# Turning the probabilities of the last self attention with ordinary matmuls instead of transposes

## The chip, the core and the metric

The kernel runs on one core of a Trainium2 chip. The metric is the device time of one execution in microseconds (us), as the median of several runs. TensorE (PE) runs the matmuls, VectorE (DVE), ScalarE (ACT) and GpSimd (POOL) the elementwise work, and DMA queues move data. PE's clock has two levels, 1.2 and 2.4 GHz; the profile gives the granted one as a share, 0.50 or 1.00, and between them as a mean over a stretch.

## What is computed

The reference is a pair of gated blocks on x [32, 100, 128] with a context [32, 1444, 128]. The last block is an attention of the tokens on themselves, a layernorm and a mixture of 8 experts. The attention is what matters here:

```python
q = (src @ Wq + bq).reshape(B, T, NHEAD, HEAD_DIM)      # T = 100, 16 heads of 8
scores = jnp.einsum('bqhd,bkhd->bhqk', q, k) * scale
probs = jax.nn.softmax(scores, axis=-1)
out = jnp.einsum('bhqk,bkhd->bqhd', probs, v).reshape(B, T, d)
return out @ Wo + bo
```

All of it is in float32.

## The kernel before

Three stages follow one another: stage A (the first block), stage B (cross attention to the context) and stage C (`stage_c`). Stage C is written by hand: each engine has its own program, and semaphores are the only tie between them. It first runs the self attention of 32 sequences and then the experts. The attention works in 8 units (`b`, 0 to 7) of 4 sequences; a sequence is two pieces of 8 heads, so there are 64 pieces (`k`) and 8 slots (`s` = `k % 8`) in a unit. A piece passes through these steps:

- PE `scores(k)` (L1801): two products of 400 columns, into one of two pairs of PSUM banks.
- DVE `subtract(k)` (L2018, L2022): the row maximum, and scores minus maximum into the tile `P`.
- ACT `exponent(k)` (L1640): exp in place in `P`.
- PE `turn_pieces(k)` (L1810): the eight 100x100 blocks of `P`, one a head, are turned into PSUM banks 4 and 5. It waits for exp of this piece and for the copy of the piece before.
- ACT `keep(k)` (L1646): one copy of all eight blocks to the tile `PT`.
- PE `weigh(k)` (L1822): eight products of `V` (with ones beside it, for the denominators) with `PT`.
- After every second piece ACT `outputs` (L1652) copies the result, PE `back` (L1847) turns it to tokens, and DVE `divide` (L2032, L2033) divides by the denominators.

PE's order in slot `s` is `scores(k + 2)`, `back` of the sequence before (even slots), `turn_pieces(k)`, one extra, `weigh(k)`. The extras prepare the next unit and finish the one before: slot 0 `gate` (L1754 on `c_YT`) and `attended` (L1766); slot 1 `turn1`; slot 2 `outer` (L1754 on `c_OT`); slot 3 `turn0` (L1749 on `c_H`); slot 4 `keys` (L1779); slot 5 `queries` (L1783); slot 6 `values` (L1754 on `c_HT`); slot 7 `turn2`. Unit 0 has none of the last unit's leftovers, unit 7 none of the next one's preparation.

ACT's order around it is `outputs`, `enter` (slot 3) or `middle` (slot 5, both four activations on L1603), `keep(k)`, `exponent(k + 1)`, then the copies of the extras. DVE's order is `divide`, `shift`, `subtract(k + 1)`, and `residual` (L2041) in slot 3. Every engine runs its list strictly in order.

`project` is the ordinary product of the kernel on four sequences, and `ident` is the identity:

```python
for j in range(GROUP):                                    # GROUP = 4
    last = mm(bank(b, T, width, j * width), lhsT[:, t.ts_(j)], rhs, start=True, stop=True)
```

Of the kernel before, what the change touches and what calls it, by code (L numbers as in the profile page):

```python
# [24 lines left out]
T = 100  # L25
# [1419 lines left out]
def stage_c(nc, t, x1, att, w1, w2, out):  # L1445

    with ExitStack() as ctx:
        def sb(name, shape, dt=F32):
            return ctx.enter_context(nc.sbuf_tensor("c_" + name, shape, dt))
# [4 lines left out]
        psum, K, tanhs, ident = t.psum, t.K, t.tanhs, t.ident  # L1454
        w, col, row, bank, tok_bank = t.w, t.col, t.row, t.bank, t.tok_bank
# [16 lines left out]
        P = sb("P", [T, 2, HQ // 2])  # L1472
# [271 lines left out]
        def _(pe):  # L1744
            mm = nc.tensor.matmul
# [59 lines left out]
            def turn_pieces(k):  # L1805
                pe.wait_ge(sem["fe_ready"], k + 1)
                if k:
                    pe.wait_ge(sem["fpT_ready"], k)
                for a in range(8):
                    x_ = nc.tensor.transpose(bank(4 + a // 4, T, T, (a % 4) * T), P[:, k % 2, t.ts_(a)], ident[0:T, 0:T])  # L1810
                x_.then_inc(sem["fpT_psum"], 1)

            def weigh(k):
# [114 lines left out]
            for k in range(PIECES):  # L1928
                b, s = divmod(k, SLOTS)
                if k + 2 < PIECES:  # L1930
                    scores(k + 2)
                if s % 2 == 0 and k:
                    back(k // 2 - 1)
                turn_pieces(k)
                if s == 0 and b >= 2:
                    gate(b - 2)
                if b < LAST:
                    if s == 0:
                        attended(b + 1)
                    if s == 3:  # L1940
                        turn0(b + 1)
                    if s == 4:
                        keys(b + 1)
                    if s == 5:
                        queries(b + 1)
                    if s == 6:
                        values(b + 1)
                if b:
                    if s == 1:
                        turn1(b - 1)  # L1950
                    if s == 2:
                        outer(b - 1)
                    if s == 7:
                        turn2(b - 1)
                weigh(k)
# [288 lines left out]
```

## Time and profile before

| | us |
|---|---|
| median of 3 runs (lowest, highest) | 2407.45 (2407.42, 2408.7) |
| the profiled execution's own time | 2401.97 |
| its span, first to last instruction | 2400.2 |
| PE busy | 2028.5 (85%) |
| DVE busy | 1583.8 (66%) |
| ACT busy | 1320.0 (55%) |
| L1810, matmul side: 512 instructions | 66.4 |
| stage C's attention loop, first turn to the last `back` | 1856.2 to 2154.4 |

An instruction group is told by its line, engine and operation and by output<-inputs; `psum<-K,c_P` is the turning of `P` with the identity, which lies in the constants `K`. A group's PE time is the busy time of overlapping instructions: eight turns in a row take 0.85 us together, though one lasts 249 ns. What stands in brackets behind a row is idle time of the engine before the row, with the instruction that ended it.

### The profile page before, as it was taken

The page shows a single profiled execution, that of the slowest core. Times are in us where ns is not written, and L with a number is a line of the kernel's source. Part 1 is how long each engine was busy: PE and PEld are TensorE (multiplying, and loading weights), DVE is VectorE, ACT ScalarE, POOL GpSimd, SP SyncE. Part 2 cuts the span into 40 slices and gives each one's busy share as a digit, 9 for nine tenths or more (in the row PEclk, how much of TensorE's full clock was granted, in tenths as well). Part 3 has the DMA queues.
Part 4 walks back from the last instruction along what each step waited for, and adds up shares of the span by engine and source line. Part 5 has one row for each costly group of instructions (what it writes and reads, how often), then busy time and mean ns, then how long its engine had stood idle before and what let it go on. Part 6 is the DMA issues. An engine that isn't in the chain of part 4 may idle for free. (4 is left out here: it accounts for less than half of the span.)

```text
span 2400.2 us, 45166 instructions
## 1 busy us (share of the span) xinstructions
PE 2028.5 (85%) x17914; PEld 1347.5 (56%) x17914; DVE 1583.8 (66%) x3854; ACT 1320.0 (55%) x2169; POOL 535.9 (22%) x476
## 2 busy tenths in 40 slices
PE   3779997466599999999999999999996888878997
PEld 2546665343355556556565555556564565656776
DVE  5844543787578878877877878878862566654443
ACT  3645554576246666666666666666673555543333
POOL 1410000553302212212222212212212233221111
PEclk9789997666589999999999999999997898879999
DMA  5026662000222313313323323313312110000000
GB/s 160 1 86 187 186 186 75 4 18 17 90 69 104 115 64 113 114 64 117 107 77 108 107 72 113 115 62 115 115 43 94 35 36 18 1 1 4 8 8 11
DMA packets 89104, 181.18 MB, mean 75 GB/s; under 512 B 5907, under 2 KB 63163, under 8 KB 88511
## 3 DMA queue, kind: packets, MB, share of 16 engines
q1 hardware_dynamic: 88894, 178.30, 22.6%
q8 instruction: 143, 2.34, 0.4%
q14 instruction: 67, 0.54, 0.1%
HBM read 95.24 MB, written 11.65 MB: 45 GB/s over the span
## 5 line engine op out<-in xcount | busy, mean ns | idle before, releaser
L1408 DVE TENSOR_REDUCE b_part_max<-psum 128x1 f32<-128x482 f32 (+3 forms) x1248 | 737.3, 650 | 187.6 <-PE psum L1285 173.6
L1198 ACT ACTIVATE b_PT<-psum 128x800 f32<-128x800 f32 x768 | 616.4, 836 | 386.0 <-PE psum L1304 380.0
L1285 PE MATMUL psum<-b_KH,b_QBD 64*128 64x482 f32 (+1 forms) x1152 | 421.4, 443 | 46.3 <-DVE b_part_max L1408 43.4
L1304 PE MATMUL psum<-b_QS,b_KS 64*128 64x200 f32 x3072 | 438.7, 288 | 0.5 <-ACT b_PT L1198 0.3
L1304 PEld LDWEIGHTS psum<-b_QS,b_KS 64*128 64x128 f32 x3072 | 339.6, 186 | 16.2 <-issue 12.1
L1320 PE MATMUL psum<-b_PT,b_V 128*32 128x200 f32 x6144 | 341.1, 339 | 0.6 <-ACT b_PT L1198 0.6
L1285 PEld LDWEIGHTS psum<-b_KH,b_QBD 64*128 64x128 f32 x1152 | 196.6, 188 | 198.0 <-DVE b_part_max L1408 118.6
L1121 POOL TENSOR_TENSOR b_KL<-b_KF,b_KH 128x1444 fp32r<-128x1444 f32 x32 | 106.8, 3337 | 691.9 <-PE psum L1304 669.7
L1320 PEld LDWEIGHTS psum<-b_PT,b_V 128*32 128x32 f32 x6144 | 159.9, 109 | 149.0 <-ACT b_PT L1198 82.3
L2096 DVE SCALAR_TENSOR_TENSOR c_U<-psum,c_gt,c_U 100x128 f32<-100x128 f32 x256 | 72.1, 344 | 129.0 <-PE psum L1917 128.8
L384 POOL TENSOR_TENSOR a_rs<-a_ve,a_half 100x4 f32<-100x4 f32 x48 | 50.0, 1041 | 420.7 <-DVE a_ve L757 420.6
L1917 PE MATMUL psum<-c_W,c_HE 128*100 128x128 f32 x1024 | 123.6, 274 | 14.1 <-ACT c_HE L1682 14.0
L1917 PEld LDWEIGHTS psum<-c_W,c_HE 128*100 128x100 f32 x1024 | 117.2, 167 | 31.8 <-ACT c_HE L1682 18.7
L1272 PE MATMUL psum<-W,b_CT 128*128 128x128 f32 (+1 forms) x768 | 117.7, 293 | 12.7 <-DVE b_part_max L1408 6.7
L804 DVE TENSOR_REDUCE a_peak<-psum 100x1 f32<-100x1446 f32 x32 | 53.2, 1664 | 105.3 <-PE psum L629 105.3
L1272 PEld LDWEIGHTS psum<-W,b_CT 128*128 128x128 f32 (+1 forms) x768 | 92.7, 188 | 41.4 <-DVE b_part_max L1408 37.4
L1682 ACT ACTIVATE c_HE<-psum,C 128x400 f32<-128x400 f32 x128 | 71.9, 587 | 78.9 <-PE psum L1906 75.9
L1646 ACT COPY c_PT<-psum 100x800 f32<-100x800 f32 x64 | 52.5, 821 | 102.0 <-PE psum L1810 102.0
L636 PE MATMUL psum<-a_P,a_CN 128*128 128x100 f32 (+1 forms) x768 | 108.0, 288 | 0.0
L1261 PE MATMUL psum<-b_CT,W 128*128 128x482 f32 (+1 forms) x192 | 101.2, 611 | 5.5 <-DVE b_QF L1382 1.5
L636 PEld LDWEIGHTS psum<-a_P,a_CN 128*128 128x128 f32 (+1 forms) x768 | 95.2, 195 | 18.7 <-issue 11.8
L1535 POOL TENSOR_TENSOR c_rs<-c_ve,c_half 100x4 f32<-100x4 f32 x24 | 24.4, 1015 | 337.0 <-DVE c_ve L1998 337.0
(274 smaller groups left out, 3204.3 us busy)
## 6 DMA issues: line engine op xcount, KB each, us to landing
b_KS<-b_KH SPq DMA_DIRECT2D x64, 722.0 KB
a_CT<-in_ctxt SPq DMA_DIRECT2D x32, 722.0 KB, 4.2
b_CT<-in_ctxt SPq DMA_DIRECT2D x32, 722.0 KB, 4.3
b_KS<-b_KL SPq DMA_DIRECT2D x32, 722.0 KB
a_CN<-in_ctxn SPq DMA_DIRECT2D x32, 704.0 KB
att_scratch<-b_AO SPq DMA_DIRECT2D x32, 200.0 KB, 1.9
c_AIN<-att_scratch SPq DMA_DIRECT2D x8, 800.0 KB
b_MB<-in_mask SPq DMA_DIRECT2D x32, 180.5 KB, 4.4
```

Source lines behind the costliest of these rows:

```text
L636: x_ = mm(bank(7, D, T, TG), CN[0:rows, m % 3, k, :], PTA[0:rows, m % 2, k, :], start=(k == 0), stop=(k == KT - 1))
L1121: pl.tensor_tensor(KL[:, :], KF[:, 0:S], KH[:, j % 2, :].bitcast(F32), ALU.subtract).then_inc(sem["kl_ready"], 1)
L1198: nc.scalar.activation(PT[:, kt % 2, 2 * a:2 * a + 2, :], psum[:, 2 * a:2 * a + 2, 0:TG], ACT.Exp).then_inc(sem["pt_ready"], 1)
L1261: m = mm(bank(b, D, size), w("xkT"), CT[:, j % 2, c:c + size], start=True, stop=True)
L1272: m = mm(bank(b, rows, D, (k % 4) * D), CT[:, j % 2, k * D:k * D + rows], w("xvT"), start=True, stop=True)
L1285: m = mm(bank(b, D, size), QBD[rows, j % 2, tile * D:(tile + 1) * D], KH[rows, j % 2, at_:at_ + size], start=True, stop=True)
L1304: m = mm(bank(p, D, 2 * T, (s % 2) * 2 * T), KS[rows, j % 2, s, kt * D:(kt + 1) * D], QS[rows, j % 2, s * 2 * T:(s + 1) * 2 * T], start=Tr ...
L1320: m = mm(psum[32 * r:32 * r + 32, 6, b * 2 * T:(b + 1) * 2 * T], V[:, j % 2, kt, 4 * b + r, :], PT[:, kt % 2, 2 * b + r // 2, (r % 2) * 2 ...
L1408: v.tensor_reduce(part_max[0:rows, q, c:c + 1], bank(b, rows, CHUNKS[c][1]), AX.X, ALU.max)\
L1682: nc.scalar.activation(HE[:, n % 2, f, :], bank((2 * n + f) % 4, D, TG), ACT.Relu, bias=t.C[:, c:c + 1]).then_inc(sem["moe_h_ready"], 1)
L1917: x_ = mm(bank(4 + n % 2, T, D, j * D), HE[:, n % 2, f, t.ts_(j)], W2[:, c * D:(c + 1) * D], start=(f == 0), stop=(f == 1))
L2096: last = v.scalar_tensor_tensor(out=U3[:, u % 2, j, :], in0=tok_bank(4 + n % 2)[:, j, :], scalar=gt[:, u, 6, j * EXPERTS + e:j * EXPERTS + ...
```

## The change

```diff
                 for a in range(8):
-                    x_ = nc.tensor.transpose(bank(4 + a // 4, T, T, (a % 4) * T), P[:, k % 2, t.ts_(a)], ident[0:T, 0:T])
+                    x_ = mm(bank(4 + a // 4, T, T, (a % 4) * T), P[:, k % 2, t.ts_(a)], ident[0:T, 0:T], start=True, stop=True)
                 x_.then_inc(sem["fpT_psum"], 1)
```

`transpose(out, in, identity)` and `matmul(out, lhsT, rhs)` both give `lhsT` transposed times `rhs`, with the block of `P` as the stationary and the identity as the moving operand. Output banks, waits, signals and the order of the work on every engine stay as they were.

## Rows read from the trace of the kernel before

**Rows 1.** Windows, PE, units 0 to 7: length, PE busy (instructions), granted clock, DMA.
```profile
1856.17:1893.85 37.68, 33.22 (x290) 0.77 0.09 28
1893.85:1929.61 35.76, 31.04 (x306) 0.90 0.09 30
1929.61:1965.81 36.20, 30.57 (x315) 0.95 0.09 30
1965.81:2003.43 37.62, 32.02 (x314) 0.91 0.09 28
2003.43:2041.39 37.96, 32.29 (x315) 0.90 0.09 29
2041.39:2081.19 39.80, 34.59 (x314) 0.84 0.00 1
2081.19:2117.89 36.70, 30.60 (x314) 0.95 0.01 2
2117.89:2154.37 36.48, 26.91 (x251) 0.71 0.01 1
```

**Rows 2.** Source lines L1810, L1754: duration of one (min/median/max, ns), first and last start.
```profile
L1810 PE MATMUL psum<-K,c_P x512: 247/249/407, 1856.2 to 2151.5; 100*100 100x100 f32 x171
...
L1754 PE MATMUL psum<-W,c_YT x64: 172/233/314, 1930.5 to 2206.4; 128*100 128x8 f32 x64
```

**Rows 3.** Timeline of PE, unit 6: start, us, what [idle before, releaser].
```profile
2082.12 0.84 PE L1754 MATMUL psum<-W,c_YT 128*100 128x8 f32 x8
...
2090.11 0.55 PE L1822 MATMUL psum<-c_PT,c_VS 100*32 100x100 f32 x16 [0.57 <-ACT c_PT L1646]
...
2093.28 1.09 PE L1754 MATMUL psum<-W,c_OT 128*100 128x128 f32 x8
...
2095.26 0.92 PE L1801 MATMUL psum<-c_KBD,c_FQ 32*100 32x400 f32 x4 [0.42 <-DVE c_P L2022]
2096.11 0.89 PE L1810 MATMUL psum<-K,c_P 100*100 100x100 f32 x8
2097.92 0.53 PE L1749 MATMUL psum<-K,c_H 100*128 100x100 f32 x4 [0.91 <-DVE c_U L2041]
...
2100.34 0.85 PE L1810 MATMUL psum<-K,c_P 100*100 100x100 f32 x8
...
2103.25 0.92 PE L1801 MATMUL psum<-c_KBD,c_FQ 32*100 32x400 f32 x4 [0.59 <-DVE c_P L2022]
2104.10 0.90 PE L1810 MATMUL psum<-K,c_P 100*100 100x100 f32 x8
...
2108.08 0.92 PE L1801 MATMUL psum<-c_KBD,c_FQ 32*100 32x400 f32 x4 [0.75 <-POOL c_KBD L1554]
```

**Rows 4.** Timeline of ACT, end of unit 4 and unit 6.
```profile
2038.94 0.87 ACT L1640 ACTIVATE c_P<-c_P 100x800 f32<-100x800 f32 x1 [0.16 <-DVE c_P L2022]
...
2097.47 0.81 ACT L1646 COPY c_PT<-psum 100x800 f32<-100x800 f32 x1
...
2105.93 0.80 ACT L1646 COPY c_PT<-psum 100x800 f32<-100x800 f32 x1
...
2107.41 0.58 ACT L1628 ACTIVATE c_FQ<-psum,xbq 128x400 f32<-128x400 f32 x1
```

**Rows 5.** Timeline of PE, units 3, 4, 7: turns of slots 4, 6; scores.
```profile
1986.45 1.54 PE L1810 MATMUL psum<-K,c_P 100*100 100x100 f32 x8
...
1995.57 0.85 PE L1810 MATMUL psum<-K,c_P 100*100 100x100 f32 x8
...
2036.17 0.92 PE L1801 MATMUL psum<-c_KBD,c_FQ 32*100 32x400 f32 x4 [0.42 <-DVE c_P L2022]
...
2122.47 1.42 PE L1801 MATMUL psum<-c_KBD,c_FQ 32*100 32x400 f32 x4 [2.26 <-DVE c_P L2022]
```

**Rows 6.** Windows, all engines (PE, PEld, DVE, ACT, POOL busy), unit 4, around a fall of the clock.
```profile
2016.94:2020.35 3.41, 2.08 (x22) 1.19 (x15) 3.34 (x8) 2.96 (x6) 0.00 (x0) 1.00 0.01 2
2020.35:2023.77 3.42, 3.42 (x27) 1.71 (x26) 1.11 (x9) 1.80 (x4) 1.01 (x1) 0.50 0.03 7
```

## The prediction

> **What bounds the kernel now.** I read first the page's slices: PE is busy through the whole span, and its clock is below full in the slices of stage C's attention. Then the windows unit by unit [rows 1]: a unit takes 35.76 to 39.80 us, PE is busy 74 to 88% of it, and the granted clock differs from unit to unit. Then the line that changes, and then three engines in order of time through unit 6, of which all but the end ran at full clock. There the reader is to see that PE is the long pole, but not alone. Its queue goes scores, turn, extra, weigh, and the turn of a piece releases the copy on ACT, for which `weigh` waits (0.57 us in slot 1 [rows 3]); where the extra is long, as `outer`, the copy is hidden and PE runs on. In four places of a unit PE waits for something that does not hang on the last turn: 0.42 us in slot 3 and 0.59 us in slot 5 for DVE's subtract, 0.91 us for DVE's residual ahead of `turn0`, 0.75 us ahead of the scores of slot 6 [rows 3], and once more 0.42 us in slot 7 [rows 5]. A longer turn eats those first.
>
> **What one turn costs.** A turn of a piece is 8 instructions, 512 over 64 pieces [rows 2]. Ordinary float32 products of this kernel show as two instructions each: `gate` and `outer` are four products in the code and x8 in the trace [rows 3], while the four transposes of `turn0` are x4. So the change makes 16 instructions of each 8. Their spacing: eight transposes take 0.85 us, the last lasts 0.249 [rows 2, 3], so (0.85 - 0.249) / 7 = 0.086 us. For ordinary products with 100 columns to load, `gate` gives (0.84 - 0.233) / 7 = 0.087, though it streams only 8. No row has an ordinary product that loads 100 and streams 100. The low end is that the second instruction hides behind the first, no cost; the high end is `outer`, loading 100 and streaming 128, at 1.09 / 8 = 0.136, so 16 x 0.136 - 0.85 = +1.3 us. I take 0.086, since load and stream are both of 100 columns as in the row that is there: 0.249 + 15 x 0.086 = 1.54 us in place of 0.85, **+0.69 us** a piece, or 44 us over 64 pieces if none were hidden.
>
> **What of it lands on the path, at full clock.** I follow one unit from the turn of slot 0, counting how late each step is.
> - Slots 0 and 1: turn, `gate`, `attended`, and turn, copy, `weigh` stand in one chain [rows 3]. +0.69 each, together +1.38.
> - Slot 2: turn and `outer` are at +2.07, but the scores of slot 3 already waited 0.42 for DVE, whose chain starts at `back` of slot 2 and is at +1.38. They start at +2.07 - 0.42 = +1.65.
> - Slot 3: the turn ends at 2097.00 + 1.65 + 0.69 = 2099.34. `turn0` waited for the residual (+1.38: 2099.30), so its 0.91 of waiting is used up. The copy, which ACT started at 2097.47 after `enter` [rows 4], now waits for the turn: 2099.38, +1.91. `weigh`, exp, `outputs` and `back` of slot 4 follow it at +1.91.
> - Slot 4: the turn ends at +2.60; the scores of slot 5 had waited 0.59, so they are at +2.01.
> - Slot 5: the turn ends at 2105.00 + 2.01 + 0.69 = 2107.70. ACT's chain (exp, keys, `middle`, copy at 2105.93) is at +1.91, so the copy starts at 2107.84: nothing lost, with 0.14 us to spare. The scores of slot 6 carry POOL's `c_KBD` as the releaser, but the code wants only the first of its four there; the queries' copy ends at 2107.41 + 0.58 = 2107.99 [rows 4], just ahead of the scores at 2108.08. It is ACT's chain again, so +1.91 and not +2.70.
> - Slots 6 and 7: +0.69 less the 0.42 in front of slot 7's scores, then +0.69, of which about 0.2 is hidden since exp of the next piece had waited for DVE (0.16 [rows 4]). Together about +0.75.
>
> The sum is +2.66 a unit instead of 5.52: half of the added work falls into waits. For units 1 to 6 that is 16.0 us. Unit 0 has no residual, `middle` or `gate`, so less is hidden (slots 1, 5 and 7 pay in full, the first turn pays double at half clock): 1.3 + 3 x 0.69 + about 0.7 = 4.1. Unit 7 pays in slots 0, 1, 3 and 7 and a part of slot 2, while slots 4 to 6 wait for DVE and ACT: 4 x 0.69 + 0.35 = 3.1. Together **+23.2 us**.
>
> **What the clock gives back.** A turn at half clock takes 1.54 us [rows 5]; 16 of the 64 last 1.3 or more. What these stretches cost is read from units 2 to 6, which do the same work. A unit at full clock: slots 0 to 3 take 2100.34 - 2081.19 = 19.15 [rows 1, 3], slots 4 and 5 take 9.12 (1986.45 to 1995.57, hardly touched by a half-clock turn in it, since ACT's chain sets it), slots 6 and 7 2003.43 - 1995.57 = 7.86 [rows 1, 5]; 36.13 in all. The five lasted 188.28, so the half clock cost them 188.28 - 180.65 = 7.6 us. A granted clock of 0.95 is a tenth of the time at half: summed over the five, 34.4 us. Each us at 1.2 GHz cost 0.22 us, because most of what PE loses there, waits absorb. Units 0, 1 and 7 have 45.7 us of it, 10.1 us by the same rate; 17.7 us in all.
>
> What did PE do before it fell? In unit 4 it was busy 2.08 of 3.41 us across slot 3, with the two waits that unit 6 shows there as 0.42 and 0.91, and then ran at 0.50 [rows 3, 6]. Falls of the middle units come in the slots where PE waits for DVE or ACT, and the change fills just these waits with matmuls: twice the instructions in the turns, and slot 3's wait of 0.91 gone. I take it that most falls of units 0 to 6 go, and that one in unit 7, where PE waits 2.26 us for DVE [rows 5], and the one at its end stay: 17.7 - 2.5 = **-15 us**.
>
> Here a rule of the Trainium skill bears on the case ("TensorE: Matmul & The Clock Gate", PE-mode transpose): a transpose does not count as a busy PE for the clock as a matmul does. This trace has no stretch that settles it: the falls lie where PE idles as well as where it turns. By the rule the falls would go for certain, since every turn becomes work that counts.
>
> The net is 23.2 - 15 = +8 us, on the profiled execution's 2401.97 (span 2400.2 and 1.8 around it): 2410. The median of the runs shown, 2407.45, is 5.5 us above that execution; the change is added to it: **2415.5 us**. My own range for this case is +3 to +14.
>
> **The rivals.**
> - All falls go, those of unit 7 too, the full-count case: 23.2 - 17.7 = +5.5, 2413. For it: every unit gets more PE work in less idle time. Against: unit 7's wait for DVE stays.
> - The falls stay, since a unit that is longer by waits elsewhere still has them. Then the 16 half-clock turns cost 1.38 and not 0.69, about half of the extra being absorbed: 23.2 + 6 = +29, 2436.5. Against: no slot gets less busy.
> - The ordinary products run at about 0.115 us, between `gate` and `outer`: +1.12 a turn. By the same walk the waits are used up in slot 3 already and slot 5's copy becomes late: +5.9 a unit, about 48 in all, less 16: +32, 2439. Against: `gate` at 0.087.
> - Faster: the recovered clock is worth more on the path than 0.22 a us. It decides from the point where the 80 us at half clock give back over 23.2 / 80 = 0.29 a us; at 0.36 it would be -6, 2401.5. For it: the timed runs are 5.5 us longer than the profiled one, which may be more half clock. Against: the five middle units, with the same work in each, say 0.22.
> - The change does nothing: the second instruction of each pair hides, and turns take what they took: 0, 2407.5. Against: `gate` and `outer` show no such hiding.
>
> **How the numbers follow.** A measurement of this kernel can tell 0.2%, 4.8 us, from no change. Forecast 0.55, of which a quarter lies under +4.8; all falls go 0.15, about half under it; falls stay 0.11; slower products 0.06; faster 0.09; nothing 0.04. Slower: 0.41 + 0.07 + 0.11 + 0.06 = 0.65. Same: 0.14 + 0.08 + 0.04 = 0.26. Faster: 0.09. The range from 2406 to 2437 holds the forecast, its two neighbours and no change, and leaves out the faster case and the slower products, 0.15.
>
> **What would show it.** L1810 with 1024 instructions and a turn of about 1.54 us at full clock; PE's waits ahead of slot 3's and slot 5's scores and of `turn0` gone or nearly so; the copy of slot 3 starting right behind its turn; units 1 to 6 about 38.8 us long with a clock near 1.00. Wrong would be: units of 36 us, a turn of 0.85 or of 2 us, a clock of 0.90 as before, or a change in the expert part, which does the same work.

## The result and the profile after

The changed kernel takes 2419.2 us in the median of 14 runs, against 2407.45 us for the kernel before in its 14. The ratio of their means is 1.0042, with an interval of 1.0029 to 1.0055, or +10 us (7 to 13). It is slower, beyond the 0.2% that can be told from no change. Run again beside other kernels it came to 1.0030 (1.0016 to 1.0045), +7 us.

The profiled execution of the changed kernel has a span of 2410.5 us, 10.3 more than before. It falls into three parts. The first turn starts at 1860.02 instead of 1856.16 (+3.9), the loop from the first turn to the last is 301.6 instead of 294.2 us long (+7.4), and the rest after the last turn's start is 248.9 instead of 249.9 (-1.0). The first part is not put down to the change (experiment e7), and the last one wanders from execution to execution as well: it is 253.7 in a second profile of the same kernel. The loop is the change, and unit by unit it reads so [rows 1 has the same of before; here a stretch begins with the first weight load of a turn, there with its first product, some 0.1 us later]. Columns: stretch, length, PE busy (instructions), granted clock, DMA.

```profile
1860.02:1897.96 37.94, 33.27 (x354) 0.96 0.09 28
1897.96:1934.89 36.93, 33.54 (x370) 1.00 0.10 29
1934.89:1973.16 38.27, 34.40 (x379) 1.00 0.09 28
1973.16:2011.42 38.26, 34.39 (x379) 1.00 0.08 28
2011.42:2049.68 38.26, 34.39 (x378) 1.00 0.09 28
2049.68:2087.94 38.26, 34.40 (x378) 1.00 0.01 1
2087.94:2126.20 38.26, 34.39 (x378) 1.00 0.01 1
2126.20:2161.62 35.42, 27.97 (x279) 0.81 0.01 2
```

Two things are to be seen. Units 2 to 6 are now alike to 0.01 us and at full clock, where before they ran from 36.20 to 39.80 with 0.84 to 0.95 [rows 1]; the time at half clock between the first and the last turn went from 75.4 to 17.1 us. The timed runs agree with the profile: the granted clock over the whole span is 0.919 to 0.929 in the 26 runs of the changed kernel, and 0.900 to 0.919 in 43 timed runs of the kernel before. And the new common length, 38.26, is longer than most of the old ones. Unit 0 still begins at half clock, and only unit 7 still falls. (Its stretch here ends at the last turn's start; the one of before between the same points is 32.55.)

The line itself, by source line (min/median/max of one in ns), first the weight loads of the kernel before, then both rows of the changed one:

```profile
L1810 PEld LDWEIGHTS psum<-K,c_P x512: 125/128/209, 1856.2 to 2151.4; 100*100 100x100 f32 x171
```

```profile
L1810 PEld LDWEIGHTS psum<-K,c_P x1024: 162/168/292, 1860.0 to 2162.9; 100*100 100x100 f32 x171
L1810 PE MATMUL psum<-K,c_P x1024: 249/252/488, 1860.0 to 2163.0; 100*100 100x100 f32 x171
```

There are 1024 instructions instead of 512. On the matmul side each is as long as before (252 ns, 249 in [rows 2]); a weight load is recorded as 168 ns instead of 128. In order of time, PE in unit 6 (start, us, what, idle before and its releaser):

```profile
2088.05 1.58 PE L1810 MATMUL psum<-K,c_P 100*100 100x100 f32 x16
2089.46 0.79 PE L1754 MATMUL psum<-W,c_YT 128*100 128x8 f32 x8
...
2095.60 1.66 PE L1810 MATMUL psum<-K,c_P 100*100 100x100 f32 x16
...
2098.17 0.55 PE L1822 MATMUL psum<-c_PT,c_VS 100*32 100x100 f32 x16 [0.57 <-ACT c_PT L1646]
...
2101.81 1.04 PE L1754 MATMUL psum<-W,c_OT 128*100 128x128 f32 x8
...
2103.37 0.92 PE L1801 MATMUL psum<-c_KBD,c_FQ 32*100 32x400 f32 x4
2104.22 1.66 PE L1810 MATMUL psum<-K,c_P 100*100 100x100 f32 x16
2105.98 0.54 PE L1749 MATMUL psum<-K,c_H 100*128 100x100 f32 x4
2106.79 0.55 PE L1822 MATMUL psum<-c_PT,c_VS 100*32 100x100 f32 x16 [0.28 <-ACT c_PT L1646]
...
2111.79 0.92 PE L1801 MATMUL psum<-c_KBD,c_FQ 32*100 32x400 f32 x4
2112.64 1.66 PE L1810 MATMUL psum<-K,c_P 100*100 100x100 f32 x16
...
2116.57 0.92 PE L1801 MATMUL psum<-c_KBD,c_FQ 32*100 32x400 f32 x4 [0.74 <-POOL c_KBD L1554]
...
2120.87 0.92 PE L1801 MATMUL psum<-c_KBD,c_FQ 32*100 32x400 f32 x4
```

Held against [rows 3, 5]: the 0.42 us ahead of slot 3's and slot 7's scores, the 0.59 ahead of slot 5's and the 0.91 ahead of `turn0` have no bracket any more, the turns have eaten them. The 0.57 us behind slot 1's turn is there as before, since the copy it waits for starts with the turn's end. So is the 0.74 ahead of slot 6's scores. ACT in the same unit:

```profile
2105.91 0.82 ACT L1646 COPY c_PT<-psum 100x800 f32<-100x800 f32 x1 [0.30 <-PE psum L1810]
...
2114.41 0.80 ACT L1646 COPY c_PT<-psum 100x800 f32<-100x800 f32 x1
...
2115.89 0.57 ACT L1628 ACTIVATE c_FQ<-psum,xbq 128x400 f32<-128x400 f32 x1
```

Slot 3's copy now waits for the turn (0.30), slot 5's does not, and the queries' copy ends at 2116.46, 0.11 ahead of slot 6's scores [rows 4]. Unit 7 on PE, where the clock falls in the wait for DVE:

```profile
2131.33 1.66 PE L1801 MATMUL psum<-c_KBD,c_FQ 32*100 32x400 f32 x4 [1.98 <-DVE c_P L2022]
2132.91 2.99 PE L1810 MATMUL psum<-K,c_P 100*100 100x100 f32 x16
```

### The profile page after: what moved, and what is told of

Its sections match the earlier page's. It is cut to its first block and busy times, and to the rows that moved or that the text cites. A ratio compares the mean times of both kernels' runs of the same rounds, so it can differ in the third digit from the quotient of the medians.

```text
span 2410.5 us, 46190 instructions
## 1 busy us (share of the span) xinstructions
PE 2055.2 (85%) x18426; PEld 1383.7 (57%) x18426; DVE 1584.2 (66%) x3854; ACT 1320.2 (55%) x2169; POOL 536.4 (22%) x476
## 5 line engine op out<-in xcount | busy, mean ns | idle before, releaser
L1304 PEld LDWEIGHTS psum<-b_QS,b_KS 64*128 64x128 f32 x3072 | 339.7, 187 | 16.2 <-issue 12.1
L1810 PEld LDWEIGHTS psum<-K,c_P 100*100 100x100 f32 x1024 | 99.6, 173 | 20.5 <-ACT c_P L1640 15.8
L1810 PE MATMUL psum<-K,c_P 100*100 100x100 f32 x1024 | 107.2, 260 | 0.7 <-ACT c_P L1640 0.7
```

The source lines that it names most:

```text
L1304: m = mm(bank(p, D, 2 * T, (s % 2) * 2 * T), KS[rows, j % 2, s, kt * D:(kt + 1) * D], QS[rows, j % 2, s * 2 * T:(s + 1) * 2 * T], start=Tr ...
L1810: x_ = mm(bank(4 + a // 4, T, T, (a % 4) * T), P[:, k % 2, t.ts_(a)], ident[0:T, 0:T], start=True, stop=True)
```

## The experiments

The theory to test has two halves: the doubled instructions cost time only in slots where the next step hangs on the turn, and the clock comes back because PE idles less. The rivals are the Trainium skill's rule on transposes ("TensorE: Matmul & The Clock Gate", PE-mode transpose), a cost that is the same wherever the turn stands, and a clock that returns nothing because other engines set the pace. Slot lengths below are between the first weight loads of two turns.

**e1: twice the transposes.** Same number of instructions as the change, but no ordinary product.

```diff
-                for a in range(8):
+                for a in [*range(8), *range(8)]:
                     x_ = nc.tensor.transpose(...)
```

> The kernel before, with every block turned twice by a transpose (16 transposes a piece, the second writing the same again). Theory: the clock came back in the changed kernel because PE works longer and waits less, whatever kind of work it is; then this kernel looks like the changed one: a turn of 1.5 to 1.7 us, units 2 to 6 of 38.2 to 38.5 us, granted clock 0.99 to 1.00 in units 1 to 6, total +6 to +13 us on the kernel before. Rival, the skill's rule that transposes do not count for the clock as matmuls do: the half-clock stretches stay, granted clock about 0.90, units of 39.5 us or more, total +20 to +30 us.

Measured: ratio 1.0017 (1.0007 to 1.0027), +4 us (2 to 7). Units 4 and 7, PE, columns as above:

```profile
2011.80:2049.74 37.94, 33.94 (x378) 1.00 0.10 29
...
2125.62:2157.39 31.77, 23.79 (x279) 0.95 0.01 2
```

Units 1 to 6 run at 1.00, with nothing but transposes in the turns. The half-clock stretches, which by that rule should have stayed, are gone; the ordinary products of a unit are those of the kernel before, now spread over 37.94 us instead of the 36.13 of a unit at full clock there. The units are 0.32 us shorter than the changed kernel's, below the band that I had given for them, and unit 7 has 3.4 us at half clock and not 13.7. So most of what the change adds to a unit (1.85 of 2.17 us over the 36.09 of e2) comes with the doubled number of instructions alone. The total, 2 to 7 us, lies at the low end of the band or below it.

**e2: transposes kept, idle PE filled.** Ordinary products of the identity with itself into 100 unused columns of PSUM bank 6.

```diff
+            def fill(n):
+                for _ in range(n):
+                    mm(bank(6, T, T, TG), ident[0:T, 0:T], ident[0:T, 0:T], start=True, stop=True)
...
+                fill(1 * {3: 2, 5: 3, 7: 2}.get(s, 0))       # ahead of scores(k + 2)
...
                 turn_pieces(k)
+                fill(1 * {3: 4}.get(s, 0))
...
+                fill(1 * {1: 2, 5: 5, 7: 2}.get(s, 0))
                 weigh(k)
```

> The kernel before with its transposes, and ordinary products of the identity with itself, whose result nobody reads, put into PE's waits of the odd slots (2 in slot 1, 6 in slot 3, 8 in slot 5, 4 in slot 7; 20 a unit, 40 instructions). Theory: half-clock stretches cost the kernel before some 15 us and go when PE idles less; the fillers lie in waits and cost nothing: units 2 to 6 of 36.0 to 36.5 us, clock 0.99 to 1.00 in units 1 to 6, total -10 to -16 us. Rival 1: the clock gives little back, since other engines set the pace: total -3 to +3 us. Rival 2: the fillers delay the path: 40 x 0.088 = 3.5 us a unit at most, total up to +10 us.

Measured: ratio 0.9963 (0.9950 to 0.9975), -9 us (-12 to -6), just short of the band. Units 3 and 6, and `attended` at the start of unit 6, here and in the kernel before:

```profile
1965.91:2002.00 36.09, 33.06 (x354) 1.00 0.09 30
...
2077.49:2115.13 37.64, 34.62 (x354) 0.95 0.01 2
```

```profile
2079.75 5.25 PE L1766 MATMUL psum<-W,c_AIN 128*100 128x128 f32 x32 [0.38 <-DVE c_gt L2059]
```

```profile
2083.33 3.71 PE L1766 MATMUL psum<-W,c_AIN 128*100 128x128 f32 x32 [0.37 <-DVE c_gt L2052]
```

Units 2 and 3 come within 0.04 us of the full-clock length worked out from the kernel before (36.13). Units 4 to 6 have one fall left, which I had not expected, in slot 0, where no filler stood: `attended` takes 5.25 us in unit 6 and 3.71 at full clock. Work that nobody reads made the kernel faster, so the half clock had been costing time, and the fillers themselves fit into the waits.

**e3 and e4: the change in some slots only.** Line 1810 with the product in slots 2 to 6 (e3), or in 0, 1 and 7 (e4), transposes in the others.

```diff
+                    if k % SLOTS in (2, 3, 4, 5, 6):          # e4: (0, 1, 7)
+                        x_ = mm(..., start=True, stop=True)
+                    else:
                         x_ = nc.tensor.transpose(...)
```

> Ordinary products for the turn in slots 2 to 6 only, transposes in 0, 1 and 7. Theory: in these slots waits for DVE and ACT take the added time (the changed kernel's slots 2 to 6 are 0.45 us longer in sum than the full-clock slots before), and the clock comes back there: units 2 to 6 of 36.4 to 37.0 us, total -6 to -11 us. Rival: the added time costs alike wherever it stands (2.13 x 5 / 8 = 1.3 us a unit): units of 37.4 us, total -4 to 0 us.

> Ordinary products for the turn in slots 0, 1 and 7 only, transposes in 2 to 6. Theory: all of these slots pay (0.44 + 0.76 + 0.50 = 1.7 us a unit in the changed kernel) and the falls of the clock in slots 3 to 6 stay in most units: units 2 to 6 of 37.8 to 39.5 us, clock 0.90 to 0.97, total +4 to +12 us, about as slow as the change as a whole with three eighths of it. Rival (alike everywhere): 0.8 us a unit, units of 37 to 38 us, total -3 to +3 us.

Measured: e3 0.9974 (0.9963 to 0.9985), -6 us (-9 to -4); e4 1.0047 (1.0033 to 1.0062), +11 us (8 to 15). Unit 4 of e3, then units 4 and 7 of e4:

```profile
2007.24:2043.77 36.53, 32.35 (x354) 1.00 0.10 30
```

```profile
2017.20:2056.44 39.24, 34.04 (x339) 0.91 0.09 28
...
2133.23:2170.01 36.78, 29.57 (x240) 0.61 0.00 1
```

Five eighths of the change make the kernel faster, and the other three eighths make it about as slow as the whole: the timed ratios don't tell e4 from the whole, and its loop is 306.7 us against 301.6. In e3 the added time is 0.44 us a unit over 36.09, 0.09 a slot, since it stands in waits, and it keeps the clock up there. In e4 the added time is on the path: slots 0, 1 and 7 at full clock are 0.43, 0.76 and 0.53 us longer than in e2. The falls of slots 3 to 6 stay. A cost that is alike everywhere is out.

**e5: transposes as fillers.** As e2, with 2 transposes for each product.

```diff
-                    mm(bank(6, T, T, TG), ident[0:T, 0:T], ident[0:T, 0:T], start=True, stop=True)
+                    nc.tensor.transpose(bank(6, T, T, TG), ident[0:T, 0:T], ident[0:T, 0:T])
```

> The filler kernel with transposes as fillers: 40 transposes of the identity a unit in the same waits, in place of 20 ordinary products (40 instructions both). Theory: the clock comes back as with ordinary fillers, since transposes keep PE as busy: units 2 to 6 of 36.0 to 37.8 us, granted clock 0.95 to 1.00, total -5 to -11 us on the kernel before. Rival, the skill's rule: fillers that are transposes do nothing for the clock, units as before (36.2 to 39.9), total -2 to +2 us.

Measured: 0.9963 (0.9944 to 0.9982), -9 us (-13 to -4), as e2. Units 3 and 5:

```profile
1966.16:2002.28 36.12, 32.90 (x355) 1.00 0.10 30
...
2040.05:2079.06 39.01, 36.01 (x355) 0.91 0.01 1
```

Transposes held the clock in units 1 to 3 just as products did; in units 4 to 6 more falls were left than in e2 (13.7 us at half clock against 10.2), and one unit, 39.01, lies outside the band. That transposes do nothing for the clock is refuted twice for this kernel, where ordinary products always stand between them; that they do exactly as much as products is not shown.

**e8: two of the eight blocks.** This tests the part of my walk that had come out too dear, the even slots.

```diff
+                    if a < 2 and k % SLOTS in (0, 1, 2, 4, 6):
+                        x_ = mm(..., start=True, stop=True)
+                    else:
                         x_ = nc.tensor.transpose(...)
```

> Only the first two of the eight blocks turned by ordinary products, in slots 0, 1, 2, 4 and 6 (two instructions more, 0.17 us). Theory: in even slots the extra behind the turn waits for divide, which has to read PSUM bank 7 first, about 0.2 us beyond the turn's last start, so slot 0 stays at 7.22 us and slots 2 and 4 at 3.87 at full clock; slot 1 has no such wait and grows from 3.94 to 4.11. Rival: every added instruction costs its 0.086 us: slot 0 at 7.39, slots 1, 2 and 4 up by 0.17 alike.

Measured in the one profile: slot 0 of units 2 to 6 is 7.22 us, as in the full-clock units of before, and slots 2 and 4 at full clock are 3.87, as there; slot 1 is 4.15, where it was 3.94. Unit 4 on PE (here L1811 is the product, L1813 the transpose):

```profile
2004.28 0.52 PE L1811 MATMUL psum<-K,c_P 100*100 100x100 f32 x4
2004.63 0.68 PE L1813 MATMUL psum<-K,c_P 100*100 100x100 f32 x6
2005.21 0.84 PE L1754 MATMUL psum<-W,c_YT 128*100 128x8 f32 x8
```

`gate` starts 0.93 us after the turn's start, as it did before (2081.19 to 2082.12 [rows 1, 3]), though two instructions were added. In even slots the extra writes PSUM bank 7, which `back` has just filled, and waits until `divide` has read it; in the kernel before `divide`'s last operation ended at 2081.97 and `gate` came 0.15 later. The profile shows no idle PE there, since the tail of the last turn still counts as busy.

**e7: the change once more.**

> The changed kernel once more, unaltered, to see whether the time from span start to the first turn (1856.2 us in the profile of before, 1860.0 in that of after) is part of the change. Theory: it is not, it wanders by some us whatever the kernel; the loop from the first turn to the last is again 301 to 303 us against 294 before, units 2 to 6 again 38.26, and the ratio lies between 1.002 and 1.005. Rival: the change makes the stages before longer too: first turn at 1860 or later and a ratio of 1.005 or more.

Measured: 1.0030 (1.0016 to 1.0045). The loop is 301.4 us, units 2 to 6 are 38.27 or 38.28, the first turn starts at 1861.9. In the ten profiles of this study it starts between 1856.2 (before) and 1865.3 (e6); of the two low ones the other is e8, 1856.7. So one sign of the rival came, a first turn after 1860, and the other, a ratio of 1.005, did not. The spread is there when stage B begins: its first work on PE comes at 631.0 us in the kernel before, 631.5 in e8, 634.8 and 636.9 in two executions of the changed kernel, behind code that is the same. From there to the first turn it is 1225.0 to 1225.3 us in all four. And e2 and e5, which turn with transposes, have the first turn at 1860.8 and 1861.1. So the 3.9 us ahead of the loop are not charged to the change.

**e6: all waits filled.** The version to which e2 points: transposes, fillers as in e2, and more in slots 0 and 2, in unit 0 and 7, and in the lead-in.

```diff
+            fill(28)
             attended(0)
+            fill(25)
             turn0(0)
...
+                if s in (0, 2) and b:
+                    fill(2, 4)                                # PSUM bank 4, ahead of back
...
                     gate(b - 2)
+                    fill(2)
```

> Transposes kept, ordinary fillers in nearly all of PE's waits of this stage: the odd slots as before, 2 products ahead of back in slots 0 and 2 and 2 behind gate, more in units 0 and 7, and in the lead-in ahead of attended, turn0, keys, queries, values. Theory: units 2 to 6 of 36.0 to 36.4 us with no fall left, units 0 and 7 shorter by 2 to 4 us each, the lead-in by 3 to 6 us: total -16 to -26 us. Rival: the falls are not what holds the units, fillers beyond those of the first filler kernel only delay: total -9 us or nearer to zero.

Measured: 0.9881 (0.9857 to 0.9904), -29 us (-34 to -23), faster than both kernels and at the fast end of my band or beyond it. The median is 2381.73 us, 26 below that of the kernel before. Units 4 and 7:

```profile
2005.60:2041.69 36.09, 34.17 (x367) 1.00 0.09 30
...
2113.88:2142.61 28.73, 26.16 (x311) 1.00 0.01 2
```

No stretch of the loop is at half clock. It lasts 277.3 us instead of 294.2: if the fillers themselves cost nothing, the 75.4 us at half clock had cost 16.8 us, 0.22 us for each. That is a mean: in slot 0 of e2's units 4 to 6, where the stretch lies almost wholly inside `attended`, 3.4 us at half clock cost 1.5 to 1.7 us, nearly a half. In the profile the way from stage B's first work to the first turn is 2.4 us shorter than in the kernel before and the part behind the loop 3.0 shorter, so with the loop it accounts for 22 us; the rest of the timed gain is not traced.

## Why the prediction came out right

The forecast was 2415.5 us, slower by 8, and the loop of the profile became 7.4 us longer; the timed difference of 7 to 13 holds both. The mechanism is the one that was forecast, a cost that waits take in part and a clock that comes back; that the sum comes within a microsecond of the loop's 7.4 is in part luck. Step by step:

- **The turn.** +0.69 us was forecast, from 0.85 to 1.54; it takes 1.58, and the spacing is (1.58 - 0.252) / 15 = 0.089, with two instructions for each product and full price for each. Neither the hidden second instruction nor the slower product happened.
- **The walk through a unit.** +2.66 us was forecast. Measured is 38.26 - 36.09 = +2.17, with the full-clock unit from e2 and e6. The waits in slots 3, 5 and 7 were eaten as forecast, and slot 5's copy did stay on ACT's chain. What I mis-sized is slot 0 (0.69), and the even slots with it: from the start of the turn to the start of `gate` it is 0.93 us before and 1.41 after, so 0.48 is paid. The wait on bank 7 hid some 0.2 us, as e8 shows, and I had not seen it because the trace shows no bracket for it. Slots 6 and 7 cost 0.55 together, where I had 0.75. Over units 0 to 6 the cost is 266.2 - 249.5 = 16.7 us (249.5 is the sum of e2's units at 34.48, 34.53 and five of 36.09), where I had 20.1.
- **The clock.** The rate of 0.22 us for each us at half clock is what e6 gives. That the falls of units 0 to 6 go and one in unit 7 stays is what happened; unit 0 still begins at half clock, and the fall at the end of unit 7 came in e7 and not in the first profile. The falls that went gave back 261.6 - 249.5 = 12.1 us in units 0 to 6 (261.6 being their length before, to the first turn of unit 7). My rate puts 13.0 of the 15.2 us there and 2.2 in unit 7.
- **Unit 7.** Its fall costs more than I had allowed: a turn at half clock now takes 2.99 us. The unit is 35.42 us long up to the last turn's start, 32.55 before and 28.73 in e6; in e1, with as many instructions but 3.4 us at half clock instead of 13.7, it is 31.77. I had +0.9 (3.1 less the 2.2), and it is +2.9.
- **The sum.** The net of units 0 to 6 is 16.7 - 12.1 = +4.6, where I had 20.1 - 13.0 = +7.1; of unit 7 it is +2.9 where I had +0.9. The cost was too high by 3.4 us, the gain by 0.9, and unit 7 too cheap by 2.0, and the errors cancelled.
- **The rule of the Trainium skill** ("TensorE: Matmul & The Clock Gate", PE-mode transpose), that transposes do not count for the clock as matmuls do, is not borne out: e1 ran units 1 to 6 at 1.00 with transposes alone in the turns. No run here has PE on transposes and nothing else. The forecast did not rest on the rule.

Open stays why the fall in slot 0 came in units 4 to 6 of e2 and not in 2 and 3, which do the same work, and whether the difference between the two ratios, 1.0042 and 1.0030, whose intervals overlap, is anything but noise.

## What to carry to other kernels

Count what an edit issues: in float32 an ordinary product was two instructions here (1024 against 512) where a transpose is one, and each had its full price of 0.089 us where the next step hangs on it. A longer step on the busiest engine costs only what the waits behind it don't take, and it may give time back by keeping PE's clock up; so walk one period slot by slot, and look in the code for waits that a pipelined PE hides from the trace. Where the clock falls inside a loop with short waits, a few useless products in these waits are worth a try: here 1.2%.

## What the runs showed of the hardware

With turns made of transposes alone the clock stayed at its upper level in units 1 to 6 of e1, as it did with products in the changed kernel. A us of PE at half clock cost 0.22 us in the mean of this loop (16.8 of 75.4), and nearly a half in e2's slot 0 (1.5 to 1.7 of 3.4), inside a run of products without a wait. The lower mean fits with PE's waits taking up the rest elsewhere. The eight instructions of `gate` took 0.79 us behind ordinary turns (2089.46 in the changed kernel) and 0.84 behind transposes [rows 3]; in e1, behind doubled transposes, they took 0.79 too, so the kind of the turn is not what makes the difference.
